# Two ends of a pipelined attention stage: start-up work moved behind the first parts, key projections and row scatters moved into the last steps

## The reference

```python
x = x + L0_xattn(layernorm(x), ctx, ctx, key_mask, Wq, bq, Wk, bk, Wv, bv, Wo, bo)   # 16 heads of 8
x = x + L0_ffn(layernorm(x), w_gate, w1, w2)                                       # 8 experts, 2 chosen per token
x = x + L1_xattn(layernorm(x), ctx, query_mask, Wq, Wkv, Wout, bout)               # 16 heads of 64
x = x + L1_ffn(layernorm(x), w1, b1, w2, b2)                                       # 128 -> 512 -> 128
```

## Time and profile before

| what | value |
|---|---|
| median of three runs | 957.94 us (957.89 to 959.22) |
| the profiled execution | 959.45 us; from its first to its last instruction 957.8 us |
| mean granted TensorE clock | 0.989 of full |
| TensorE matmul busy | 897.3 us (94%) |
| VectorE, ScalarE, Pool busy | 674.9 us (70%), 695.8 us (73%), 447.5 us (47%) |
| first attention stage | to about 356 us |
| experts | from about 371 us |

### The profile page before, as it was taken

One profiled execution on the slowest core, in us unless ns is written; L12 is line 12 of the kernel. 1 busy time (PEld: TensorE's weight loads), 2 busy tenths in 40 slices (PEclk: granted clock), 3 DMA queues, 4 the chain that ended last, 5 costly groups with the idle time before them and its releaser, 6 DMA issues. The chain is left out here.

```text
span 957.8 us, 29951 instructions
## 1 busy us (share of the span) xinstructions
PE 897.3 (94%) x8399; PEld 786.6 (82%) x8399; DVE 674.9 (70%) x2145; ACT 695.8 (73%) x2694; POOL 447.5 (47%) x739
## 2 busy tenths in 40 slices
PE   3899999999999969999998799999999999999996
PEld 2677776777766759999997699999999999999995
DVE  5688888888888873222222788888787778777873
ACT  1898888888888944333334999998788878887882
POOL 4033433433433453111114777776666666666542
PEclk9999999999999989999999999999999999999998
DMA  4676667666666612222222111222112111211110
GB/s 138 215 228 195 197 203 213 198 205 200 211 212 206 195 42 89 66 69 71 69 74 69 35 62 62 63 66 64 53 53 66 60 50 54 66 60 55 44 51 10
DMA packets 113563, 103.93 MB, mean 109 GB/s; under 512 B 11761, under 2 KB 100627, under 8 KB 113494
## 3 DMA queue, kind: packets, MB, share of 16 engines
q1 hardware_dynamic: 106594, 88.81, 29.6%
q0 software_dynamic: 6112, 13.90, 4.7%
q10 hardware_dynamic: 788, 0.39, 0.1%
HBM read 56.53 MB, written 46.53 MB: 108 GB/s over the span
## 5 line engine op out<-in xcount | busy, mean ns | idle before, releaser
L643 ACT ACTIVATE PR<-PR,nmx 128x128 f32<-128x128 f32 x512 | 198.1, 390 | 8.2 <-DVE nmx L843 5.8
L643 ACT ACTIVATE PR<-bank,nmx 128x128 f32<-128x128 f32 x512 | 182.6, 385 | 7.8 <-issue 7.3
L334 POOL TENSOR_TENSOR PR<-PR,rden 128x512 f32<-128x512 f32 x128 | 133.9, 1046 | 92.0 <-DVE rden L848 85.6
L1123 PE MATMUL bank<-ident,PR 128*128 128x128 f32 x1024 | 156.6, 276 | 4.3 <-POOL PR L334 1.7
L1123 PEld LDWEIGHTS bank<-ident,PR 128*128 128x128 f32 x1024 | 118.6, 141 | 48.6 <-issue 40.8
L643 ACT ACTIVATION_READ_ACCUMULATOR PR<-bank,nmx 128x1 f32 x512 | 114.9, 224 | 0.0
L735 ACT ACTIVATE H<-bank 128x512 f32<-128x512 f32 x70 | 41.8, 597 | 90.4 <-PE bank L1308 90.4
L1333 PE MATMUL bank<-XCT,wqk 128*128 128x128 f32 x832 | 103.7, 278 | 0.7 <-ACT XCT L631 0.7
L1333 PEld LDWEIGHTS bank<-XCT,wqk 128*128 128x128 f32 x832 | 96.9, 192 | 3.5 <-ACT XCT L631 1.0
L643 ACT ACTIVATION_READ_ACCUMULATOR PR<-PR,nmx 128x1 f32 x512 | 96.9, 189 | 0.0
L843 DVE TENSOR_REDUCE nmx<-bank 128x4 f32<-128x512 f32 x128 | 86.6, 677 | 14.7 <-PE bank L1141 13.7
(11 more groups left out here) (195 smaller groups left out, 2096.7 us busy)
## 6 DMA issues: line engine op xcount, KB each, us to landing
second_layer_values<-wide SPq DMA_DIRECT2D x32, 512.0 KB, 3.0
wide<-second_layer_values SPq DMA_DIRECT2D x32, 512.0 KB
expert_outputs<-HF SPq DMA_DIRECT2D x32, 256.0 KB
expert_outputs<-HF SPq DMA_DIRECT2D x64, 128.0 KB, 1.9
KBD<-expert_outputs SPq DMA_DIRECT2D x128, 64.0 KB
QS<-expert_outputs SPq DMA_DIRECT2D x32, 256.0 KB
PR<-expert_inputs SPq DMA_DIRECT2D x36, 128.0 KB, 2.0
expert_outputs<-PR POOLq DMA_DIRECT2D x35, 128.0 KB, 2.0
```

What stands on the lines that cost most here:

```text
L334: nc.gpsimd.tensor_tensor(unit, unit, rden[:, p, G * g:G * g + G].unsqueeze(2).broadcast_to([P, G, P]), ALU.mult).then_inc(s["nm"], 1)
L643: last = nc.scalar.activation(PR[:, g, j * P:(j + 1) * P], scored, ACT.Exp, bias=nmx[:, p, h:h + 1], accum_out=den[:, p, h:h + 1])
L1123: last = nc.tensor.transpose(T_BANK[g % 2][:, j * P:(j + 1) * P], PR[:, g, j * P:(j + 1) * P], ident[:])
```

## The change

It does the following, in the first steps (n from -3 to 2):

- Pool's memset of `mk_rows` waits for the first normalised sequence (`a["xn"]`).
- On SyncE in step -1, the context load of sequence 2, the three bias row transfers (before: end of step -2) and the two early loads stand behind `KBD` and `QS` of sequence 0, in that order and, for the early loads, at the end of the step.
- On VectorE `bias_rows` moves from step -2 to step -1, behind the `ql` of that step. In steps 0, 1 and 2 `weights_and_masks` stands behind `ql` too. The copies of transposed Wv and Wo and the first mask part move from step -1 to step 0; the second mask part is cut in two, for sequences 4 to 15 in step 1 and 16 to 31 in step 2.
- TensorE transposes Wv and Wo at the head of step 0 and waits there for their copies and the first mask part.

In the last steps (n from 32 to 35):

- TensorE turns five contexts in step 32 (into banks 0 and 6), and projects the keys of sequences 0 and 1 in step 33 and of sequence 2 in step 34, into banks 6 and 1. After the steps only the keys of sequences 3 and 4 are left. The nine reads of the table stand in threes: behind the keys of 3, between the halves of 4, and behind them.
- ScalarE copies contexts and the keys of 0 to 2 before it scales Wq and copies the query mask.
- In step 34 Pool scatters the rows of sequence 30 before it keeps those of 31.

```diff
@@ SyncE
+            def move_bias_rows():
+                sp.wait_ge(rows_zeroed, 1)
+                sp.wait_ge(parts_ready, 1)
+                for r in range(3):
+                    sp.dma_start(brow[r:r + 1, :, :], brow_b[0:1, :, r, :]).then_inc(rows_moved, 16)
             def step0(n, p):
-                if exists(n + 3):
+                starting = isinstance(n, int) and n < 0
+                if exists(n + 3) and not (starting and n == -1):
                     load_ctx(sp, a, n + 3, q)
-                if isinstance(n, int):
+                if isinstance(n, int) and n != -1:
                     early_loads(n)
...
+                if starting and n == -1:
+                    load_ctx(sp, a, 2, q)
+                    move_bias_rows()
...
-                if isinstance(n, int) and n == -2:
-                    (the two waits and three transfers of move_bias_rows)
+                if starting and n == -1:
+                    early_loads(n)
@@ Pool
                 if n == -3:
+                    pool.wait_ge(a["xn"], 1)
                     nc.gpsimd.memset(mk_rows[:].bitcast(FP32), 0.0).then_inc(rows_zeroed, 1)
...
+                if not is_sequence(NB + 2, n):
+                    keep_rows(n - 3, q)
+                    scatter_rows(n - 4, p)
+                else:
+                    scatter_rows(n - 4, p)
+                    keep_rows(n - 3, q)
@@ ScalarE, after the steps
+            read_contexts(0, KEYS_A - 4, bank[0], bank[6])
+            for m in range(3):
+                read_keys(m, 0)
+                read_keys(m, 1)
             act.wait_ge(ld_w1, 12 * 16)
             nc.scalar.activation(wqk1[:, 0, :], wqk1[:, 0, :], ACT.Copy, scale=float(DH1) ** -0.5).then_inc(wq_scaled, 1)
             act.wait_ge(wo_strips, 2)
             nc.scalar.activation(fill_q[:], bank[0][:, 0:NB], ACT.Copy).then_inc(parts_ready, 1)
+            read_keys(3, 0)
+            read_keys(3, 1)
             act.wait_ge(rt["counts"], 2)
             nc.scalar.activation(egap[:], gap[:], ACT.Exp).then_inc(rt["egap"], 1)
+            read_keys(4, 0)
+            read_keys(4, 1)
@@ VectorE
                 if n == -1:
+                    dve.wait_ge(ld_x1, 16)
+                if n == 0:
                     dve.wait_ge(set_pe, 2)
...
                 if n == 1:
-                    nc.vector.tensor_scalar(mk_rows[0:3, 4 * P:], mk3[0:3, 4 * P:], -1.0, pcol[0:3, 0:1],
+                    nc.vector.tensor_scalar(mk_rows[0:3, 4 * P:16 * P], mk3[0:3, 4 * P:16 * P], -1.0, pcol[0:3, 0:1],
+                                            ALU.add, ALU.mult)
+                if n == 2:
+                    nc.vector.tensor_scalar(mk_rows[0:3, 16 * P:], mk3[0:3, 16 * P:], -1.0, pcol[0:3, 0:1],
                                             ALU.add, ALU.mult).then_inc(set_copy, 1)
...
-                if isinstance(n, int):
+                if isinstance(n, int) and n not in (0, 1, 2):
                     weights_and_masks(n)
...
+                if isinstance(n, int) and n == -1:
+                    bias_rows()
+                if isinstance(n, int) and n in (0, 1, 2):
+                    weights_and_masks(n)
@@ TensorE
                 if n == 0:
-                    pe.wait_ge(set_copy, 2)
-                if n == -1:
                     pe.wait_ge(ld_w2, 32)
...
+                    pe.wait_ge(set_copy, 2)
...
+                if is_sequence(NB + 1, n):
+                    project_keys(0, 0)
+                    project_keys(0, 1)
...
+                if is_sequence(NB, n):
+                    pe.wait_ge(a["e"], NU * NB)
+                    pe.wait_ge(a["pjv"], 2 * NB)
+                    turn_contexts(0, CTX_A, bank[0], bank[6])
+                    pe.wait_ge(ld_w1, 12 * 16)
+                if is_sequence(NB + 1, n) or is_sequence(NB + 2, n):
+                    project_keys(n - NB, 0)
+                    project_keys(n - NB, 1)
...
+            project_keys(3, 0)
+            project_keys(3, 1)
+            for k in range(3):
+                load_starts(k)
+            project_keys(4, 0)
+            for k in range(3, 6):
+                load_starts(k)
+            project_keys(4, 1)
+            for k in range(6, NE):
+                load_starts(k)
```

More of the change, by code:

```diff
@@ L547, in late_constants, with keep_rows, scatter_rows @@
                                             pattern=[[1, P]], channel_multiplier=-1).then_inc(rows_zeroed, 1)
+            def keep_rows(m, p):
+                if exists(m):
+                    wait_apart(pool, (rt["xn"], m + 1), *([(rt[f"sc{p}"], 2 * loads(m - 2, p))] if exists(m - 2) else []))
+                    nc.gpsimd.tensor_copy(XK[:, p, :], XND[:]).then_inc(rt["kept"], 1)
+            def scatter_rows(m, p):
+                if exists(m):
+                    for k in range(2):
+                        wait_apart(pool, (rt["placed"], m + 1), (rt["kept"], m + 1))
+                        nc.gpsimd.indirect_dma_start(xs, bass.IndirectOffsetOnAxis(scat_idx[:, p, k:k + 1], 0), XK[:, p, :],
+                                                     None).then_inc(rt[f"sc{p}"], 16)
             def step0(n, p):
@@ L1317, in _ @@
             total = starts[NE]
-            keys_ahead(1, KEYS_A, KEYS_AHEAD, CTX_B, bank[6], (bank[0], bank[1]))
+            turn_contexts(1, CTX_B, bank[3], bank[6])
+            for m in range(KEYS_A, KEYS_AHEAD):
+                project_keys(m, 0)
+                project_keys(m, 1)
             pe.wait_ge(wq_scaled, 1)
```

85 lines of the change are left out of this document (30 added, 55 removed).

## The result

| what | before | after |
|---|---|---|
| median on one chip, 18 runs each | 958.87 us | 955.68 us |
| ratio to before, 95% interval | | 0.9969 (0.996 to 0.9978) |
| profiled execution | 959.45 us, span 957.8 us | 956.81 us, span 955.2 us |

The kernel is 3.0 us (2.1 to 3.8) faster; 8.0 were forecast. Two further comparisons with fresh runs of the same kernel, `after_again` and `after_third`, gave 0.9954 (0.994 to 0.9968) and 0.9964 (0.9952 to 0.9977): 3 to 4 us, about half of the forecast. The chips differ by 2% in speed (before took 943 us on two of them, 960 on the others), so all that follows is compared by its ratio to the kernel before on the same chip.

The account below looks back on a forecast made before the run. TensorE was taken as the bound, busy 94.8 of 100 us in the loop, with gains only where it idles: first steps -4.8, last steps -3.2, together -8.0, from median 957.94 to 949.9 us (range 946.0 to 954.0).

Parts of the forecast that it names:

- First scores at 19.45, held by the mask part: Start: sequence 0's first scores at 19.45 in place of 23.55, waiting for VectorE's mask part and not QS; -4.1 us.
- Covered by 0.8 us: Start: scores of sequence 1 possible at 28.3, needed at 29.1, so its QS would arrive 0.8 us before it is needed.
- Earlier full pace, -0.5: Start: TensorE's matmuls, at half pace until about 28.9, return to full pace earlier; 0 to 0.8 us, taken as -0.5.
- Mask pieces, 1.0 and 1.27 us for -0.2: Steps 1 and 2: the 2.07 us mask operation, cut into pieces of 1.0 and 1.27 us, nets -0.2 us.
- The loop is left earlier by what it is entered earlier: First layer's loop: bodies unchanged, so the head start, -4.8 us, is kept through to its end.
- Last counts 1.2 us later: Last steps: keys and transposes moved ahead in TensorE's queue delay the last counts and the tile table by 1.2 us (bounds 0 and 4).
- the rival with keys at 1.2 GHz: Last steps: clock falls at 350, 5.3 us of keys run low, last steps give only -0.5; 952.6 us, chance 0.14.
- Nine reads at 0.45 each: Last steps: TensorE's tile table reads take 4.1 us in all, ending at 366.4; experts' first transpose at 366.7, -3.9 us.
- +0.7 for a low clock into the experts: Last steps: clock falls in TensorE's idle time and slows some 1.5 us of expert work, costing 0.7 us.
- only small starts: Rival: XN of sequence 1 still blocked, scores at 20.4, second mask piece costs 1.27; first steps -2.0; 952.7 us, chance 0.15.
- Slower by TensorE's pace: Rival: half pace at the start gives back 2.05 us, 1.2 GHz from 350 into the experts; +2.1, 960.0 us, chance 0.05.
- The 0.05 rival: Rival: stores or loads priced at 0 eat the head start, last steps only trade waits; 957.9 us, chance 0.05.

Follow-up runs that it names:

- spare: The changed kernel with 23 spare matmuls on TensorE, results unused, before the table's reads and between the first of them: ratio 0.9974 to before.
- keys4_first: The changed kernel with both halves of the fifth sequence's keys ahead of all nine table reads: ratio 0.997 to before.
- ctx_split: The changed kernel with the loop's one load of five contexts cut into five loads, one in each of five steps: ratio 0.9956 to before.
- loads_late2: The changed kernel with the bulk loads of steps -1 to 3 (masks, X) issued behind KBD and QS: ratio 0.9936 to before, median 954.09 us.
- one_piece: The changed kernel with bulk loads behind KBD and QS, and all 3584 mask columns made in one operation in step 1: ratio 0.9925 to before.
- tail_only: The kernel before with only the last steps' half of the change: ratio 0.9981 to before, 1.8 us faster.

## Why the prediction was wrong

Right in sign, and too high by more than half. By its steps:

- **First scores at 19.45, held by the mask part: held.** 19.21, with the bracket naming L849. Its parts too: XN of sequence 1 at 11.79 (11.8), the Q difference of sequence 0 at 12.31 (12.1). QS of sequence 0 was issued at 16.27, not 15.1 (15.03 in `spare`), and for the first scores that was covered. By the Trainium skill, SBUF — State Buffer, section "Who interferes with whom", VectorE and Pool can hold each other up on the port pair that they share: the trace agrees once more, in that the first XN, out of the memset's way, took 0.35 us in place of 1.80, and the cast that now lies beside the KBD memset took 1.34.
- **"Covered by 0.8 us": this is the first step that failed.** I had it as what is late next, and put Q of sequence 1 at 25.2 by adding durations of issues, and its landing at the 3.08 of the earlier trace rows. The issue came at 26.32 and the landing 4.35 later: 2.4 us more against a cover of 0.8, and behind the wait 3.4 to 6.8 us of matmuls at half pace. 1.1 of it is the cast that meets the memset, and is missing in `spare`, `keys4_first` and `ctx_split`; the 1.3 of the landing are in all, and more. It was priced from one row with a DMA share of 0.78, while the change puts the mask loads beside the context and X right ahead of this transfer (1.04). With these loads behind it, in `loads_late2`, there is no wait and the median is 2.8 us lower.
- **Earlier full pace, -0.5: fell.** The clock was at the low level from 19.9 and again from about 30.1, 3.4 us each in after, where the kernel before had its slow matmuls for 5.3 us in one stretch.
- **Mask pieces, 1.0 and 1.27 us for -0.2: held** in size (1.00 and 1.27). Their worth is too small to be told: in `one_piece` 0.8 was won and 0.8 given back, and the times don't part.
- **"The loop is left earlier by what it is entered earlier": not quite.** From sequence 11 to 13 after lost 1.6 and 0.8 us of its lead. What was lost lies at a wait for QS: 0.60 us in the profile before, 1.27 with 3.4 us of low clock behind it in after, 1.50 without in `after_third`. `tail_only`, with the old start, has it too, so the change's start didn't make it, and the one profile of before may have been a lucky one.
- **Last counts 1.2 us later: held.** They stand at 356.08 for 355.8, with a lead of 0.8 at sequence 30: 1.1 later. The keys of the third sequence ran at full clock and took 2.05 us (1.85 by the sum), and the clock was up over all three, so the rival with keys at 1.2 GHz fell; it had taken the wrong keys. Those of the fifth sequence did run low. The pool's new order was priced at 0; no run tells it apart.
- **Nine reads at 0.45 each: the second step that failed, by its size.** From 361.4 to 367.1 are eight distances, 0.71 each; the two rows that were added up, the load and its arithmetic, leave out 0.25 us between them and to the next. In `keys4_first`, where no matmul stands between the reads, the distance is 0.70 (343.8 to 349.4). 6.4 for the nine in place of 4.1 is 2.3 us, the amount by which the first transpose missed its place (1.8 won from sequence 30, 3.9 forecast, 2.1 short). The floor of about 600 ns for such a read, in the Trainium skill, DMA: Bandwidth & Descriptors, section "Latency and other measured facts", was nearer than the 0.45 of the rows: by it the nine take 5.4 us (an estimate from the page), where the trace has 6.4. That the sum by it, -1.9 for the last steps, lies by the measured -1.8 and -1.6 is in part luck: 0.7 of it stood for a low clock in the experts, and to the first transpose it gives -2.6.
- **+0.7 for a low clock into the experts: fell in after and `after_third`, not everywhere.** There the stretch ended at 368.0, a moment ahead of the first transpose. In `ctx_split`, whose last steps have the same text, it ran 5.5 us into the experts, whose first transpose stands at 368.51:

```profile
363.50:374.00 10.50, 9.12 (x39) 8.17 (x40) 2.52 (x9) 2.29 (x4) 3.68 (x6) 0.51 0.35 107
```
- **The rivals.** The nearest in time, *only small starts* (952.7), is not what took place: the start was as large as forecast and was lost behind. *Slower by TensorE's pace* had the right mechanism, half pace behind the new start, with the wrong cause: it gave back 2.05 us of the start, where 1.9 to 3.5 were lost by sequence 3, and its loss at the end did not come. The 0.05 rival, a head start eaten in the next steps by loads priced at 0, with last steps that only trade waits (957.9), was nearest to the mechanism in its first half; its price, the whole gain, was too high, and it named no transfer. None named a late Q as the loss, though the text had it as next. Two sums among them don't come out of the terms given. For *only small starts*, -3.1 for the scores, -0.5 for the pace and at most +0.2 for the mask rows give -3.4 and not -2.0 (-2.3 with the 1.27 set against them whole); for *the clock stays up*, -4.1, -0.8 and -0.2 give -5.1 and not -5.7. Neither changes the forecast.

The terms of the sum in short, from the profiles: first steps -2.5 and -0.8 (forecast -4.8), the loop +1.7 and -0.1 from sequence 3 to 30, last steps -1.8 and -1.6 (-3.9 to this point). What stays open: why the low stretch behind Q of sequence 1 is 3.4 us in one execution of the kernel and 6.8 in another, which is the 1.7 us between their outputs of sequence 0; and whether the low clock after 500 us has anything to do with these edits.

## What to carry to other kernels

When work is moved out of the way of one critical transfer, look where it lands in the same queue: it is now ahead of the next one, and that one's landing must be priced with the moved bytes in flight, not by a row from before the move. Where a sum is built from rows of a sequencer, take the distance between starts and not the sum of the durations. And where a wait of 2 us stands in a busy stretch, put down the slower clock behind it as well.

## What the runs showed of the hardware

- Reads of an SBUF value into a TensorE register: 0.30 to 0.56 us for the load, 0.15 for the arithmetic, and 0.70 to 0.73 us from one to the next in after, `spare` and `keys4_first`.
- The read back of Q, 256 KB, took 3.1 to 5.0 us from its issue to the matmul that waited for it: 3.1 and 3.2 at a DMA share of 0.78, 3.9 at 0.89, 4.4 to 5.0 at 1.04 to 1.11.
- TensorE's granted clock fell to the 1.2 GHz level for 3.4 to 6.8 us in the middle of dense work, behind waits of 1.3 to 2.7 us; behind one of 1.37 us and one of 1.50 us it did not fall. In the same kernel and place it fell in some executions and not in others.
- One transfer of five contexts in the loop made the step beside it 1.6 us longer on average than five transfers of one context (14 and 4 executions).
- A cast of 0.25 us on VectorE that meets a memset of 1.8 us on Pool took 1.3 to 2.1 us. Whether the cast or the operation behind it was hit differed between kernels with the same start and moved the first read back by 1.1 us: with the mask rows landed by 7.7 us the cast was hit, with a landing at 8.1 us or later it was not.
